# One SBUF residue for the wide TensorE operands, and three changed orders, in a decoder layer of two programs

## The reference

```python
x = layernorm(x + attention(x))     # linear attention, 16 heads of 32
x = layernorm(x + cross(x, ctx))    # rmsnorm, W_in, plus a row of a 64-row table per token
x = layernorm(x + ffn(x))           # x and weight rounded to fp6 in blocks of 32, one 512x512 product

# attention: p = (x @ W.T + b) per head @ proj, features (cos p, sin p); 128 map columns
kv  = einsum('blhm,blhd->bhmd', k_features, v)
out = einsum('blhm,bhmd->blhd', q_features, kv) @ Wo.T + bo
```

## Time and profile before

| | before |
|---|---|
| median of 3 runs | 1644.85 us (1642.84 to 1645.97) |
| the profiled execution: its own time, and its span | 1645.52 us, 1643.5 us |
| busy PE (matmul), DVE, ACT, POOL | 1584.3, 1199.0, 1113.3, 708.8 us |
| mean granted clock of TensorE | 0.988 of 2.4 GHz |

### The profile page before, as it was taken

The page is one execution under the profiler, slowest core; times in us unless marked ns, Lnnn a source line. Parts: engine busy times, 40 slices in busy tenths (PEclk is TensorE's granted clock), DMA queues, the critical chain, the costliest instruction groups (busy, mean ns, idle before and its releaser), DMA issues. The chain is left out here.

```text
span 1643.5 us, 29746 instructions
## 1 busy us (share of the span) xinstructions
PE 1584.3 (96%) x11188; PEld 1120.7 (68%) x11188; DVE 1199.0 (73%) x1849; ACT 1113.3 (68%) x1450; POOL 708.8 (43%) x633
## 2 busy tenths in 40 slices
PE   7999999999999999999999999998799999999995
PEld 5656766676676667667666766754577787778784
DVE  5577677758757766875776686888678777777775
ACT  5696677668667767866877786678146665666563
POOL 4233115103412410440341053463188878897884
PEclk9999999999999999999999999999899999999997
DMA  5100102201210220220022022001612222222211
GB/s 171 53 26 14 65 1 79 78 1 39 80 39 1 78 78 2 71 83 3 2 78 78 1 78 78 27 27 52 164 46 83 84 78 83 78 88 78 76 40 51
DMA packets 49176, 95.77 MB, mean 58 GB/s; under 512 B 3552, under 2 KB 3872, under 8 KB 49056
## 3 DMA queue, kind: packets, MB, share of 16 engines
q1 hardware_dynamic: 39776, 76.67, 14.8%
q10 hardware_dynamic: 9280, 17.31, 2.9%
HBM read 60.38 MB, written 33.59 MB: 57 GB/s over the span
## 5 line engine op out<-in xcount | busy, mean ns | idle before, releaser
L793 DVE SCALAR_TENSOR_TENSOR feat<-feat,phases 128x1024 f32<-128x1024 f32 x256 | 300.8, 1216 | 173.4 <-ACT feat L683 173.2
L683 ACT ACTIVATE feat<-phases 128x1024 f32<-128x1024 f32 x256 | 248.4, 1024 | 138.5 <-PE phases L533 118.1
L690 ACT ACTIVATE feat<-feat 128x1024 f32<-128x1024 f32 x256 | 271.7, 1062 | 69.0 <-DVE feat L793 60.3
L396 POOL TENSOR_TENSOR xt_hi<-xt_raw,singles 128x512 fp32r<-128x512 f32 x60 | 67.9, 1162 | 493.0 <-PE bank L525 464.2
L696 ACT ACTIVATE feat<-feat 128x1024 f32<-128x1024 f32 x256 | 256.0, 1045 | 5.0 <-DVE feat L800 4.7
L800 DVE TENSOR_SCALAR feat<-feat 128x1024 int32<-128x1024 int32 x256 | 199.3, 781 | 48.4 <-ACT feat L690 47.8
L418 POOL TENSOR_TENSOR res<-res,bo_all 128x512 f32<-128x512 f32 x60 | 73.6, 1251 | 205.3 <-DMA res<-x 205.0
L595 PE MATMUL kv_sum<-feat,v 128*32 128x256 f32 x2048 | 123.8, 382 | 0.0
L621 PE MATMUL kv_sum<-feat,kv_cols 128*32 128x512 f32 x1024 | 123.1, 598 | 0.0
L523 PE MATMUL bank<-xt_hi,win_hi 128*128 128x512 f32 x256 | 108.7, 425 | 8.3 <-DVE win_lo L745 8.3
L1305 ACT ACTIVATE xs<-xs,shift,rstd 128x512 f32<-128x512 f32 x96 | 71.5, 806 | 61.8 <-POOL shift L1168 61.8
(11 more groups left out here) (219 smaller groups left out, 3620.5 us busy)
## 6 DMA issues: line engine op xcount, KB each, us to landing
normed<-res SPq DMA_DIRECT2D x32, 513.0 KB, 4.3
xt_raw<-xT SPq DMA_DIRECT2D x15, 1024.0 KB, 7.1
res<-x SPq DMA_DIRECT2D x30, 512.0 KB, 4.2
xs<-normed SPq DMA_DIRECT2D x24, 513.0 KB, 3.9
out<-xs ACTq DMA_DIRECT2D x24, 512.0 KB, 2.8
feat<-normed SPq DMA_DIRECT2D x8, 513.0 KB, 3.9
out<-feat ACTq DMA_DIRECT2D x8, 512.0 KB, 2.8
xt_raw<-ctx SPq DMA_DIRECT2D x8, 256.0 KB, 3.5
```

The source lines that it names most:

```text
L683: act.activation(feat[2 * (w % 2) + p][:, 0, :], phases[:, 2 * p:2 * p + 2, :].rearrange("p h n -> p (h n)"), ACT.Identity, bias=ROUND).th ...
L690: act.activation(f[:, 1, :], f[:, 0, :], ACT.Sin, scale=-TWO_PI).then_inc(sin_done, 1)
L793: dve.scalar_tensor_tensor(f[:, 0, :], f[:, 0, :], ROUND, phases[:, 2 * p:2 * p + 2, :].rearrange("p h n -> p (h n)"), ALU.subtract, ALU.s ...
```

## The change

**Places.** The `sb` lines are put in another order, in both programs. Small tensors now stand together, ahead of the wide ones in a number that fills them up to one residue, or behind them. No tensor changes its size, and no instruction is added or removed. Start addresses modulo 256, worked out from the sizes in the order of the lines:

| wide tensor | before | after |
|---|---|---|
| `win`, `wf`, `fold`, `feat0`, `feat1` (all of `Kept`) | 128 | 128 |
| `wq`, `wo`, `proj_hi`, `proj_lo` | 192 | 128 |
| `xt`, `stack`/`keys`, `v`, `feat2`, `feat3`, `att`, `res` | 96 | 128 |
| `turn`, `back`, `scaled`, `grid`, `quantised` | 64 | 128 |
| `chosen`, `table_parts1` | 96, 192 | 128 |
| `xs2`, `xs3`, ... | 128, 160, ... | 128, 160, ... |

**Orders.** (1) Opening: step K(0, 3) now stands ahead of `sin(1)`. (2) Border: `parts` now stands behind `stats(1)`. (3) Close, second slot: `scale` -1 moves from the end to the front, and `quant` -2 moves behind `means`.

```diff
--- before.py
+++ after.py
@@ -137,7 +137,7 @@
     after = {
         0: [V(0, 0), sin(0), K(0, 2), cos(0), V(0, 1)],
-        1: [sin(1), K(0, 3), cos(1), V(0, 2), V(0, 3), V(1, 0), kv(0)],
+        1: [K(0, 3), sin(1), cos(1), V(0, 2), V(0, 3), V(1, 0), kv(0)],
@@ -150,7 +150,7 @@
-             ("repeats",), ("context",), W(1, 1), W(1, 2), ("table",), W(1, 3), ("parts",), stats(1), norm(1, 0), norm(1, 1)],
+             ("repeats",), ("context",), W(1, 1), W(1, 2), ("table",), W(1, 3), stats(1), ("parts",), norm(1, 0), norm(1, 1)],
@@ -177,20 +177,21 @@
+        columns = sb("columns", [P, 3, KD])
+        half_power = sb("half_power", [P, 2, TPC])
+        eps = sb("eps", [P, 2, TPC])
+        singles = sb("singles", [P, 8])
+        zero, ones_row = singles[:, 0:1], singles[0:PATCHES, 1:2]
+        moments = sb("moments", [P, TPC, 2])
         whi = {"k": kept.win_hi, "v": kept.wf_hi, "q": sb("wq_hi", [P, KD, D], F32R), "o": sb("wo_hi", [P, KD, D], F32R)}
...
-        columns = sb("columns", [P, 3, KD])
...
-        half_power = sb("half_power", [P, 2, TPC])
-        eps = sb("eps", [P, 2, TPC])
-        singles = sb("singles", [P, 8])
@@ -208,9 +209,9 @@
+        scratch = sb("scratch", [P, 2, D])
         res = sb("res", [P, TPC, ROW])
         stats = sb("stats", [P, TPC, 6])
-        moments = sb("moments", [P, TPC, 2])
@@ -970,8 +970,8 @@
-        [("bias", -3), ("quant", -2), ("means", 0), ("norms", 0), ("ffn", -3, 0), ("ffn", -3, 1),
-         ("back", -2, 0), ("back", -2, 1), ("scale", -1)],
+        [("bias", -3), ("scale", -1), ("means", 0), ("quant", -2), ("norms", 0), ("ffn", -3, 0), ("ffn", -3, 1),
+         ("back", -2, 0), ("back", -2, 1)],
@@ -1036,7 +1037,6 @@
-        xs = [*kept.first_rows, *(sb(f"xs{r}", [P, PAIR, ROW])[:] for r in range(len(kept.first_rows), RING))]
         turn_hi = [sb(f"turn_hi{n}", [P, KD * P], F32R) for n in TILES]
         turn_lo = [sb(f"turn_lo{n}", [P, KD * P], F32R) for n in TILES]
...
         table_parts = [kept.fold[:, 0:D].bitcast(F32R), *(sb(f"table_parts{b}", [P, D], F32R)[:] for b in range(1, BODY_BATCHES))]
+        xs = [*kept.first_rows, *(sb(f"xs{r}", [P, PAIR, ROW])[:] for r in range(len(kept.first_rows), RING))]
+        rms_eps = sb("rms_eps", [PATCHES, 1])
+        sums = [sb(f"sums{r}", [P, 2 * PAIR]) for r in range(2)]
```

More of the change, by code:

```diff
@@ L189, in attention @@
         ident, ends = kept.ident, kept.ends
-        half_power = sb("half_power", [P, 2, TPC])
-        eps = sb("eps", [P, 2, TPC])
-        singles = sb("singles", [P, 8])
-        zero, ones_row = singles[:, 0:1], singles[0:PATCHES, 1:2]
         xt_hi = [sb(f"xt_hi{c}", [P, KD, CHUNK], F32R) for c in range(CHUNKS)]
@@ L238, in attention @@
         stage = {"v": in_rows(feat[3]), "k": in_rows(feat[1]), "q": query_stage[:], "o": res[:, :, 0:D]}
-        scratch = sb("scratch", [P, 2, D])
         w_in = {m: sem(f"w{m}_in") for m in "vkqo"}
@@ L1021, in context_and_quantised @@
         b_in_all, g_init_all, decay, patch_of_row = kept.kv_cols[:, 0, :], kept.kv_cols[0:PATCHES, 1, :], kept.decay, kept.patch_of_row
+        minus_half = sb("minus_half", [P, 2 * PAIR])
+        eps4 = sb("eps4", [P, 2 * PAIR])
+        neg_mean = sb("neg_mean", [P, 2 * PAIR])
+        neg_part = sb("neg_part", [P, 2 * PAIR])
+        shifted = sb("shifted", [P, 2 * PAIR])
+        rstd = sb("rstd", [P, 2 * PAIR])
         bf_all = sb("bf_all", [P, D])
@@ L1024, in context_and_quantised @@
         ones = sb("ones", [PATCHES, P], BF16)
[L1025 to L1029, removed]
         bank = [ps(f"bank2_{r}", [P, D]) for r in range(4)]
@@ L1046, in context_and_quantised @@
         quantised = sb("quantised", [P, PAIR * D])
[L1047 to L1050, removed]
         centred = [sb(f"centred{n}", [P, D]) for n in range(2 * PAIR)]
-        shifted = sb("shifted", [P, 2 * PAIR])
-        rstd = sb("rstd", [P, 2 * PAIR])
-        shift = sb("shift", [P, 2 * PAIR])
         at_end = sb("at_end", [PATCHES, SEQ], BF16)
@@ L1058, in context_and_quantised @@
         squares = sb("squares", [PATCHES, DCTX])
-        shifted_square, mean_square, ctx_inv = sb("shifted_square", [PATCHES, 1]), sb("mean_square", [PATCHES, 1]), sb("ctx_inv", [PATCHES, 1])
         patch = sb("patch", [PATCHES, D])
@@ L1062, in context_and_quantised @@
         table_parts = [kept.fold[:, 0:D].bitcast(F32R), *(sb(f"table_parts{b}", [P, D], F32R)[:] for b in range(1, BODY_BATCHES))]
+        xs = [*kept.first_rows, *(sb(f"xs{r}", [P, PAIR, ROW])[:] for r in range(len(kept.first_rows), RING))]
+        rms_eps = sb("rms_eps", [PATCHES, 1])
+        sums = [sb(f"sums{r}", [P, 2 * PAIR]) for r in range(2)]
+        var = sb("var", [P, 2 * PAIR])
+        scale = [sb(f"scale{r}", [P, PAIR * NBLK]) for r in range(2)]
+        inv = sb("inv", [P, PAIR * NBLK])
+        shift = sb("shift", [P, 2 * PAIR])
+        shifted_square, mean_square, ctx_inv = sb("shifted_square", [PATCHES, 1]), sb("mean_square", [PATCHES, 1]), sb("ctx_inv", [PATCHES, 1])
         x_loaded, context_in = kept.x_loaded, kept.context_in
```

## The result

| | before | after | predicted |
|---|---|---|---|
| median of 6 runs each, same chip | 1643.98 us (1641.55 to 1645.97) | 1631.41 us (1627.09 to 1633.40) | 1629 us |
| ratio of the medians, 95% interval | | 0.9924 [0.991, 0.9938] | |
| profiled execution: own time, span | 1645.52, 1643.5 us | 1629.87, 1627.5 us | |

What follows compares the result with a forecast made beforehand. PE's wide-matmul pace was taken to bound some 1,400 us; only the ends and border had deciding waits. From 1645.5 us, -8.4 (places) - 3.4 - 0.7 - 3.5 = -16.0 gave 1629.5, 1629 for the median; range 1610 to 1642.

Steps and rivals of the forecast that it cites:

- No duration of an instruction is changed: Both programs: program text changes no instruction's duration, so the only question is whether PE's pace depends on start addresses.
- Case B: Rival for the whole kernel: places do nothing, only the orders count; 1638 us, chance 0.28.
- multiples of 64 as the good case: Wide matmuls: operands at multiples of 64 allow the faster pace, 228.8 against 233.8 ns; residue 96 never holds it.
- Case C: Rival: equal residues never reach the faster pace, and the second program loses 4.2 us; 1642 us, chance 0.09.
- case D: Rival: equal residues make the two reads meet in each step, 5.0 ns on 4,200 steps; 1659 us, chance 0.06.
- The 3.0 ns a step: First program's wide matmuls: 0.6 x 5.0 ns saved on each of 2,800 steps, 8.4 us off.
- Case E: Rival: wide steps all alike, another 5.0 ns below 228.8 on 4,200 steps; 1600 us, chance 0.09.
- over some 1,400 us the time is PE's pace, and what another engine gains there is worth nothing: Bodies of both programs, 100 to 1090 and 1210 to 1600 us: PE bounds; only ends and border have deciding waits.
- the cover that cost DVE, ACT and POOL at nothing: Both windows: these engines' new addresses cost nothing; a DVE pass would need to become a quarter slower.
- Opening, -3.4: Opening: K(0, 3)'s bias ahead of the masks removes PE's 1.9 us wait and 1.5 us of lower clock.
- Border, -0.7: Border: `parts` fits into DVE's wait for POOL's power, moving the chain to the first transpose forward by 0.69 us.
- Close, -3.5: Close: PE transposes pair -1 1.8 us earlier and at full clock; 3.9 us counted, 3.5 taken.

Runs made afterwards that it cites:

- orders alone (2): The three orders (opening, border, close) with the old places, against the kernel before: 1635.24 us, ratio 0.9957.
- places alone (1): The new places with the three old orders, against the kernel before: 1637.65 us, ratio 0.9963.
- all at 160 (3): The changed kernel with every wide operand moved 32 bytes on, to residue 160: 1632.78 us, ratio to before 0.9928.
- unequal (4): The changed kernel with wide tensors at unequal multiples of 64 (64 and 128; second program 128 and 192): 1643.54 us, ratio to before 1.0005.
- unequal (5): The changed kernel with wq, wo at 64 and xt, att, win, wf at 128; second program 128 and 0: 1644.83 us, ratio to before 1.0003.
- Q first (12): The changed kernel with the Q product ahead of its sine in slots 9 to 13 of the loop: 1613.79 us, ratio to before 0.9817.
- experiments 6: The changed kernel without the third matmul of each Q product block, outside the first sequence: 1624.21 us, ratio to before 0.9884.
- experiment 8: The changed kernel with ACT's first sine over 32 of 1,024 columns in the query half: 1608.78 us, ratio to before 0.979.

## Why the first program gave its gain back

The period of a sequence falls from phase product to phase product. In the third sequence most of the key slots became 0.10 us shorter (8.77 to 8.67), and slot 13 became 0.64 longer (12.17 to 12.81), slots 9 and 12 0.2 each. In all, the key half went from 70.1 to 69.3 us and the query half from 71.0 to 71.8. A faster PE would not by itself make the query half longer; something in the chain of ACT and DVE became slower. It stands at slot 9, where POOL begins to split the next tokens (line 396) beside DVE's masks. Before, then after:

```profile
383.05 5.02 POOL L396 TENSOR_TENSOR xt_hi<-xt_raw,singles 128x512 fp32r<-128x512 f32 x4 [66.53 <-PE bank L525]
384.03 0.69 DVE L800 TENSOR_SCALAR feat<-feat 128x1024 int32<-128x1024 int32 x1
...
385.16 1.01 DVE L800 TENSOR_SCALAR feat<-feat 128x1024 int32<-128x1024 int32 x1 [0.44 <-ACT feat L690]
```

and after:

```profile
378.00 4.93 POOL L396 TENSOR_TENSOR xt_hi<-xt_raw,singles 128x512 fp32r<-128x512 f32 x4 [64.59 <-PE bank L525]
...
379.05 2.99 DVE L800 TENSOR_SCALAR feat<-feat 128x1024 int32<-128x1024 int32 x2
```

Before, the first mask starts 0.98 us behind POOL's start, just ahead of POOL's second operation, and takes 0.69 us. POOL's second operation then takes 1.58 us, where it takes 1.04 when undisturbed. After, the mask starts 1.05 us behind, when POOL's second operation has begun; that one takes 1.04 us, and each of the two masks about 1.5. The pair takes 2.99 us and not 385.16 + 1.01 - 384.03 = 2.14. So DVE reaches the next pair's subtraction (line 793) 10.04 us behind the one before it, not 8.95; a longer row at line 855 (1.23 us, before 0.72) beside POOL adds to that. The steps of ACT and DVE are then 0.6 to 1.1 us later behind PE's phase products than before, up to slot 13, where PE waits for `stack_lo`: 0.54 us before at 418.47, 1.33 after at 414.44.

```profile
417.68 0.74 DVE L814 SCALAR_TENSOR_TENSOR stack_lo<-bank,columns,stack_hi 128x512 fp32r<-128x512 f32 x1
...
418.47 0.50 PE L523 MATMUL bank<-wo_hi,att_hi 128*128 128x512 f32 x1 [0.54 <-DVE stack_lo L814]
```

and after:

```profile
413.65 0.74 DVE L814 SCALAR_TENSOR_TENSOR stack_lo<-bank,columns,stack_hi 128x512 fp32r<-128x512 f32 x1
...
414.44 0.51 PE L523 MATMUL bank<-wo_hi,att_hi 128*128 128x512 f32 x1 [1.33 <-DVE stack_lo L814]
```

It repeats. The table gives means over sequences 2 to 7, and for their six first masks at slot 9 the start behind POOL's split and the duration, in us:

| kernel | key half | query half | mask starts | mask takes |
|---|---|---|---|---|
| before | 70.1 | 71.2 | 0.98 | 0.69 |
| orders alone (2) | 70.1 | 71.2 | 0.98 | 0.69 to 0.70 |
| after | 69.3 | 72.1 | 1.01 to 1.06 | 1.53 to 1.57 |
| places alone (1) | 69.3 | 72.1 | 1.02 to 1.07 | 1.52 to 1.57 |
| all at 160 (3) | 69.3 | 72.7 | 1.05 to 1.06 | 1.53 to 1.54 |
| unequal (4) | 69.7 | 72.2 | 1.05 to 1.06 | 1.53 to 1.54 |
| unequal (5) | 69.5 | 72.4 | 1.03 to 1.04 | 1.56 |
| Q first (12) | 69.3 | 69.6 | 1.63 to 1.64 | 0.95 to 0.96 |

In each trace POOL's second operation starts at 1.00. The kernels whose mask starts ahead of it keep a query half of 71.2 us; the others with the same order have 0.9 to 1.5 us more. All masks of slot 9 together take 14.5 us before and 24.0 after, so this slot holds nearly all of what line 800 grew by. Experiment 12 has long masks as well (its second one takes 1.46 to 1.47 us), but the Q product's split stands ahead of them, and PE's wait is mostly gone.

This also bears on why experiments 4 and 5, with paces between, ended where before did. Their query half is 1.0 and 1.2 us a sequence longer than before, and the key half only 0.4 and 0.7 shorter. In the second program the stretch up to the transposes of pair -3 is 3.8 and 2.3 us longer than before, by its slower steps (233.2 and 232.4). The two losses use up what the orders gave at the ends. The collision thus is seen in the rows and goes with the long query half in each kernel that has slots 9 to 13 in their old order; no run moves POOL's split by itself, so that it is the whole of the give-back is not shown.

The Trainium skill ("SBUF — State Buffer", section "SBUF: two separate sides") describes the port pair that DVE and GpSimd share as an exclusive lock for certain forms of DVE operations: whichever starts first holds it for the whole instruction. The rows agree with it in kind: who started first kept its usual time, the mask 0.69 us before and POOL's operation 1.04 after, and the other took longer, 1.58 and 1.54 us. A shift of 0.07 us at the start decided it. Whether this form of mask should need the lock, no run here tells apart.

## Why the prediction was right or wrong

- **The sign and the size: right, and the size by luck.** 1629 was predicted and 1631 measured. In the profiled executions the first program's body brought 0.2 us and not 9.1; the missing 8.9 came from the second program (5.8, no term), the opening (1.2 more than said) and the close (1.9 more).
- **"No duration of an instruction is changed ... whether PE's pace depends on start addresses": right.** It does, and experiments 1 and 2 part it from the orders. Case B (1638, places do nothing) fell.
- **The reason was wrong.** The prediction took multiples of 64 as the good case. What counts is the distance between the two operands: 160 beside 160 is as fast as 128 beside 128 (experiment 3), and 64 beside 128 gives 229.6 to 230.8 ns one way round and 233.1 to 233.3, hardly anything, the other (before, 4, 5). Case C, equal residues as the pair that never reaches the faster pace, and case D are refuted: no distance is faster than equal residues, though for Q 64 below is as fast.
- **The 3.0 ns a step were too few.** Measured: 2.6 for K, 3.5 for Q, 6.3 for V, 5.6 for W, and 1.7 and 2.9 in the second program, which the sum had at nothing. In PE work that is 15.9 us, against 8.4 foreseen and 16.8 as the outer bound. Case E (1600) fell: no kind moved by more than 6.3 ns. The 216 ns of the Trainium skill ("TensorE: Matmul & The Clock Gate", section "Back-to-back issue gap"), from which the prediction worked out 1566 us, is there the gap of a single matmul by itself; no kind here came below 226.9.
- **The step that failed in the mechanism: "over some 1,400 us the time is PE's pace, and what another engine gains there is worth nothing", and with it the cover that cost DVE, ACT and POOL at nothing.** A PE that is busy for 99% of the window still waited at one place per sequence, 5.6 us in all, for a chain through ACT and DVE. In the query half that chain sets the time (experiments 6 and 8). That a faster PE then only waits longer, and that a DVE mask can be moved against a POOL operation, 9.5 us of new waits together, was in no term. PE saved nothing in the query half: it grew by 0.9 us a sequence.
- **Opening, -3.4 against -4.6.** The wait and the fall of the clock went as said. Experiment 1, with the old order, had a wait of 0.95 us and no fall of the clock at 36 us, and reached the third phase product at 41.23 us, 1.8 behind after. With the old places the new order brought more: 40.27 us in experiment 2, 3.8 ahead of before. So the order is worth 1.8 to 3.8 us, by one execution of each; the larger figure holds a wait of 1.90 us and a lower clock behind it (granted 0.57 from 36 to 40 us, against 1.00 in experiment 1).
- **Border, -0.7 against -0.2.** From the last statistics row's start to the first transpose it was 7.28 us before and is 7.08. POOL's power took 1.51 us beside line 880 and 1.01 before, so 0.5 of the 0.69 us came back as its longer time.
- **Close, -3.5 against -5.4.** Experiment 1 with the old order took 43.38 us, all kernels with the new one 36.9 to 37.6. `quant` of -2 took 6.6 us where 7.1 were said, and that of -1 5.2 where 6.5 were: its first row takes 0.69 us, not 1.75 as in the earlier trace rows, since POOL's bias (line 1179), which ran beside it before from 1617.01 us, is done by then, as foreseen. PE's idle time ahead of -2 grew by 3.2 us, where 3.7 were said. One stretch of half clock (granted 0.51 from 1602.8 to 1606.2 us) now begins within the transposes of -2, and at those of -1 the clock is whole, as said.

## What to carry to other kernels

Where streamed matmuls with weight loads set the pace, try moving and stationary operands at the same start modulo 256, by ordering the allocations: here it took 0.7 to 2.7% off a wide step, and places alone 0.37% off the kernel. Then ask for each stretch what is second: a share of busy time of 99% doesn't say that a faster engine will bring anything, and the one wait that repeats in each turn of the loop does. A bias or split that frees a bank belongs ahead of long element-wise work on the same engine. That order in slots 9 to 13 was worth more (18 us) than the whole change, and left the query half at 69.6 us, near the 69.2 of experiment 8, which leaves out most of ACT's sines there.

## What was not expected of the hardware

- A wide matmul step takes 226.9 to 234.0 ns by the distance of its two start addresses, and the sign counts: stationary 64 below moving gives 229.6 to 230.8, 64 above 233.1 to 233.3. With equal residues K and Q (moving `xt`) stay at 230.3 to 231.1 while V and W reach 227 to 228, and 64 beside 64 gives 229.4 (W) and 230.3 (Q). Why stays open; the distance isn't all.
- A mask took 0.69 us when it began 0.98 us behind the start of POOL's split, and 1.52 to 1.57 when it began 1.01 to 1.07 behind, in all 42 cases of sequences 2 to 7 in seven kernels. POOL's second operation begins at 1.00.
